# Normalised rows made, turned and stored in the message stage, and loaded as columns by the last stage

## The reference

```python
x = x + _L0_gnn_ref(_layernorm(x), edge_index, ...)
x = x + _L0_ffn_ref(_layernorm(x)[None], ...)[0]

def _L0_gnn_ref(x, ...):                       # H = 4 heads of C = 64, edges sorted by dst
    h = (x @ W).reshape(n, H, C)
    alpha = leaky_relu(a_src[src] + a_dst[dst])           # self loops included
    alpha = exp(alpha - segment_max(alpha, dst)[dst])
    alpha = alpha / (segment_sum(alpha, dst)[dst] + 1e-16)
    out = segment_sum(alpha[:, :, None] * h[src], dst) + bias
    return relu(layernorm(out) * ln_gamma + ln_beta)

def _L0_ffn_ref(x, ...):                       # B = 1: one routing decision for all rows
    logits = jnp.mean(x, axis=1) @ Wr + br     # the two best of 8 experts, for every row the same
    h = gelu(einsum('nd,edf->enf', x, W1) + b1)            # F = 512
    y = einsum('enf,efd->end', h, W2) + b2
    out = sum of the two chosen experts' y by their weights
    return layer_norm(out + x) * gamma + beta
```

## Time and profile before

| | |
|---|---|
| time, median of 3 runs (lowest, highest) | 3611.67 us (3609.06, 3613.48) |
| the profiled execution's own time | 3606.3 us |
| its span, first to last instruction | 3604.6 us |
| mean granted TensorE clock | 0.812 |
| PE busy | 2428.7 us (67%) |
| DVE busy | 2371.9 us (66%) |
| POOL busy | 1617.3 us (45%) |
| ACT busy | 1529.1 us (42%) |
| HBM read and written | 352.42 and 43.43 MB |

### The profile page before, as it was taken

How to read it: one execution, slowest core, us unless ns; L and a number is a source line. 1 busy time by engine, 2 the same in 40 slices (tenths; PEclk the granted TensorE clock), 3 DMA queues, 4 the chain that set the end, 5 groups by cost and what they waited for, 6 DMA issues and landing times. The chain is left out here.

```text
span 3604.6 us, 63268 instructions
## 1 busy us (share of the span) xinstructions
PE 2428.7 (67%) x12504; PEld 1741.4 (48%) x12504; DVE 2371.9 (66%) x9742; ACT 1529.1 (42%) x4803; POOL 1617.3 (45%) x1701
## 2 busy tenths in 40 slices
PE   8545556555665665665565556565565589999998
PEld 6434444444444444444444444444444356666666
DVE  6446766766766766766676766676676645566555
ACT  5334444544444544544444544444444321222211
POOL 0265665655665665665565655655655100000000
PEclk9857777777777777777877777777777799999999
DMA  7644444444444444444444444444444211111110
GB/s 206 191 119 125 130 126 124 128 125 125 127 128 123 130 127 124 128 128 124 127 127 125 129 124 126 132 122 124 134 125 122 48 56 35 35 35 35 41 41 32
DMA packets 237623, 397.71 MB, mean 110 GB/s; under 512 B 66609, under 2 KB 167729, under 8 KB 237425
## 3 DMA queue, kind: packets, MB, share of 16 engines
q0 software_dynamic: 80544, 229.59, 23.2%
q1 hardware_dynamic: 155674, 165.33, 15.0%
q10 hardware_dynamic: 1207, 1.09, 0.1%
HBM read 352.42 MB, written 43.43 MB: 110 GB/s over the span
## 5 line engine op out<-in xcount | busy, mean ns | idle before, releaser
L643 POOL DMA_INDIRECT rows<-table,idx x1666 | 1599.0, 960 | 1073.3 <-issue 471.5
L736 PE MATMUL bank<-msg,oh 128*128 128x260 f32 x3332 | 1091.9, 483 | 175.9 <-issue 125.4
L736 PEld LDWEIGHTS bank<-msg,oh 128*128 128x128 f32 x3332 | 789.1, 246 | 367.9 <-issue 205.2
L938 ACT ACTIVATE msg<-rows,we 128x65 f32<-128x65 f32 x1904 | 478.5, 333 | 0.4
L1195 DVE TENSOR_TENSOR msg<-rows,bank 128x520 f32<-128x520 f32 x595 | 377.2, 686 | 1.1 <-ACT carry L958 0.9
L756 PE MATMUL bank<-ident,lastmax 70*128 70x70 f32 x240 | 70.6, 388 | 403.8 <-DVE lastmax L1273 354.5
L829 PE MATMUL bank<-rows,msg 128*128 128x256 f32 x1536 | 340.6, 378 | 0.0
L816 PE MATMUL bank<-rows 128*128 128x512 f32 x768 | 336.3, 595 | 4.8 <-DMA rows<-in_L_ffn_W 4.8
L829 PEld LDWEIGHTS bank<-rows,msg 128*128 128x128 f32 x1536 | 288.4, 189 | 51.4 <-issue 10.6
L761 PE MATMUL bank<-ident_b,ohT 128*128 128x128 bf16 x1680 | 195.8, 306 | 161.6 <-DVE adsh L1297 69.1
L1009 ACT ACTIVATE ln<-mv,eps 128x1 f32<-128x1 f32 x119 | 35.1, 295 | 621.7 <-DVE mv L1344 454.3
(11 more groups left out here) (200 smaller groups left out, 3360.8 us busy)
## 6 DMA issues: line engine op xcount, KB each, us to landing
dst_b<-dst SPq DMA_DIRECT2D x122, 448.0 KB
rows<-table,idx POOLq DMA_INDIRECT x1666
tab_w<-table SPq DMA_DIRECT2D x121, 134.5 KB
x_w<-in_x_rows SPq DMA_DIRECT2D x121, 128.0 KB
x_mid<-x_o SPq DMA_DIRECT2D x119, 128.0 KB
table<-msg SPq DMA_DIRECT2D x50, 269.0 KB, 3.1
rows<-x_mid SPq DMA_DIRECT2D x26, 512.0 KB, 3.9
msg<-in_x_rows SPq DMA_DIRECT2D x51, 256.0 KB, 3.2
```

Of the source, the lines that this page charges most:

```text
L643: pool.indirect_dma_start(rows[:, slot, t, :], None, table, bass.IndirectOffsetOnAxis(ap=idx[slot][:, t:t + 1], axis=0), bounds_check=None ...
L736: mm = pe.matmul(psA, oh[:, of, t, :], msg[:, of, t, :], start=(t == 0), stop=(t == TILES - 1))
L938: ins = act.activation(head_cols(msg[:, s, t, :])[:, h, :], head_cols(rows[:, at.slot(), t, 0:HC1])[:, h, :], ACT.Copy, scale=we[:, t, h:h ...
```

## The change

Window by window, the message stage now makes the normalised rows itself (`xn`), turns them, and stores them as columns in a new HBM array `xn_t` (256 x 12,800). The last stage loads a group's columns from it in place of turning rows. The pieces of the diff are, in order: the lists of DVE, ACT and PE; the two PSUM places; XN on DVE; XNT on PE, behind `lastT^`, and a wait ahead of `router`; XNT on ACT, behind `oh*`; the store on SP, at the end of its step; and in the last stage the load on SP (one group ahead), PE's group, and DVE's copy.

```diff
-            wcur^ r_sc newseg^ r_mn node^ r_d1 r_d pen^ NODE_V* RUNMAX^ NOHAS* LASTMAX^ MTILE* ohT0^ MNODE* AD* MAXSELF* ohT^ ZN*
+            wcur^ r_sc newseg^ r_mn node^ r_d1 r_d pen^ NODE_V* RUNMAX^ NOHAS* LASTMAX^ XN MTILE* ohT0^ MNODE* AD* MAXSELF* ohT^ ZN*
...
-        act2 = Ticks(sem("act2"), """oh_b* we we_act carry msgs0 asrc^ msgs rexp acc carried oh* wself ln2 y2 lhs ln1 y1""", 6)
-        pe2 = Ticks(sem("pe2"), "nodemax* agg lT^ lastT^ turned^ expand* half router carry", 6)
+        act2 = Ticks(sem("act2"), """oh_b* we we_act ln2 y2 lhs carry msgs0 asrc^ msgs rexp acc carried oh* XNT wself ln1 y1""", 6)
+        pe2 = Ticks(sem("pe2"), "nodemax* agg lT^ lastT^ XNT turned^ expand* half router carry", 6)
...
+        psN = [bank[5][:, 512 - P:], bank[7][:, 512 - P:]]
...
+            def normed_rows(s):
+                return dve.scalar_tensor_tensor(out=xn[:, :], in0=x_o[:, s, 0:D], scalar=x_o[:, s, D:D + 1],
+                                                in1=ln2[:, 3:4].to_broadcast([P, D]), op0=ALU.subtract, op1=ALU.mult)
...
+                if before:
+                    act2.wait(dve, "y2", at)
+                    pe2.wait(dve, "XNT", at, -1)
+                mark(before, "XN", lambda: normed_rows(s))
...
+                if before:
+                    dve2.wait(pe, "XN", at)
+                    act2.wait(pe, "carry", at)
+                    act2.wait(pe, "XNT", at, -1)
+                    for k in range(KD):
+                        mm = pe.transpose(psN[k], xn[:, k * P:(k + 1) * P], ident[:, :])
+                    pe2.mark("XNT", mm)
...
+                if before:
+                    act2.wait(pe, "XNT", at)
...
+                if before:
+                    pe2.wait(act, "XNT", at)
+                    act.wait_ge(s_turned, at.k * (16 * RING) + 16 * (at.off - 2 + XPADS))
+                    for k in range(KD):
+                        ins = act.activation(xnT[:, k, :], psN[k], ACT.Copy)
+                    act2.mark("XNT", ins)
...
+            def store_turned(at, lead):
+                w = sp.value_load(step_tab[0:1, 0, bass.ds(at.number(lead), 1)], min_val=0, max_val=N)
+                sp.dma_start(xn_t[:, bass.ds(w, P)].rearrange("(k p) n -> p k n", p=P), xnT[:, :, :])\
+                  .then_inc(s_turned, 16)
...
+                if before:
+                    act2.wait(sp, "XNT", at)
+                    hold(sp, s_sp_held)
+                    store_turned(at, -2)
...
+            def load_transposed(at, lead):
+                sp.dma_start(fxT[:, at.slot(lead), :, :],
+                             xn_t[:, bass.ds(at.number(lead) * GROUP, GROUP)].rearrange("(k p) n -> p k n", p=P))\
+                  .then_inc(s_fxT[at.slot(lead)], 16)
...
             def group(at):
-                dve3.wait(pe, "xT", at, -1)
+                pe.wait_ge(s_fxT[at.slot()], at.landed(1))
...
-                    if q == QB // 2:
-                        pe3.mark("half", mm)
-                        transpose_rows(at, 1)
...
-            def move_transposed(at, lead):
-                s = at.slot(lead)
-                pe3.wait(dve, "xT", at, lead - 1)
-                for k in range(KD):
-                    ins = dve.tensor_copy(fxT[:, s, k, :], psF[k])
-                dve3.mark("xT", ins)
```

More of the change, by code:

```diff
@@ L144, in build @@
     XO_ROWS = (GROUPS + 1) * GROUP
+    XT_COLS = GROUPS * GROUP
+    XPADS = KD * -(-(XT_COLS - N) // D)
+    assert N + P <= XT_COLS and XPADS > 0
     with ExitStack() as ctx:
@@ L239, in build @@
         x_o = sb("x_o", [P, 2, D + 2])
+        xn = sb("xn", [P, D])
+        xnT = sb("xnT", [P, KD, P])
         zrow = sb("zrow", [1, D + 1])
@@ L306, in build @@
         s_mid = sem("s_mid")
+        s_turned = sem("s_turned")
+        s_fxT = [sem(f"s_fxT{i}") for i in range(2)]
         s_fwr = sem("s_fwr")
@@ L347, in build @@
         act3 = Ticks(sem("act3"), " ".join(HID), 2)
-        pe3 = Ticks(sem("pe3"), " ".join(HID) + " half xT out", 2)
+        pe3 = Ticks(sem("pe3"), " ".join(HID) + " out", 2)
         sp3 = Ticks(sem("sp3"), "stored", 3)
@@ L549, in _ @@
             step(over_last, -2, -1)
+            fin_act.wait(sp, "XNT", fin)
+            hold(sp, s_sp_held)
+            store_turned(over_last, -1)
+            load_transposed(At(0, 2, 0), 0)
             for slot in range(RING):
@@ L570, in _ @@
             hold(sp, s_sp_held)
+            sp.wait_ge(s_turned, total * 16 + 16 * XPADS)
+            hold(sp, s_sp_held)
             sp3.credit(sp)
@@ L763, in step @@
                 else:
-                    pe2.skip(pe, ["lT^", "lastT^", "turned^"], at)
+                    pe2.skip(pe, ["turned^"], at)
                 if ahead:
@@ L859, in _ @@
             pe.drain().then_inc(s_once, 1)
+            fin_dve.wait(pe, "XN", fin)
+            for k in range(KD):
+                mm = pe.transpose(psN_last[:, k * P:(k + 1) * P], xn[:, k * P:(k + 1) * P], ident[:, :])
+            fin_pe.mark("XNT", mm)
             pe.wait_ge(s_setup, N_MEAN)
@@ L889, in _ @@
                 act.dma_start(x_mid[r:r + n, :], zeros[0:n, :]).then_inc(s_tab[i] if i < PAIR_RING else s_pad, 16)
+            for c in range(N, XT_COLS, D):
+                n = min(D, XT_COLS - c)
+                for k in range(KD):
+                    act.dma_start(xn_t[k * P:(k + 1) * P, c:c + n], zeros[:, 0:n]).then_inc(s_turned, 16)
             act.wait_ge(s_pool, 6)
@@ L996, in step @@
                     act2.skip(act, ["oh*"], at)
+                if before:
+                    pe2.wait(act, "XNT", at)
+                    act.wait_ge(s_turned, at.k * (16 * RING) + 16 * (at.off - 2 + XPADS))
+                    for k in range(KD):
+                        ins = act.activation(xnT[:, k, :], psN[k], ACT.Copy)
+                    act2.mark("XNT", ins)
+                else:
+                    act2.skip(act, ["XNT"], at)
                 if prev:
@@ L1026, in _ @@
             fin_act.mark("lhs", act.activation(m_lhs[:, 0:1], mask[:, 2:3], ACT.Copy, scale=ln2[:, 3:4]))
+            fin_pe.wait(act, "XNT", fin)
+            act.wait_ge(s_turned, total * 16 + 16 * (XPADS - 1))
+            fin_act.mark("XNT", act.activation(xnT[:, :, :].rearrange("p k n -> p (k n)"), psN_last, ACT.Copy))
             for n in N_EXP:
@@ L1456, in _ @@
             step(over_last, -2, -1)
-            move_transposed(At(0, 2, 0), 0)
             dve3.rest(dve, DVE3_A)
+            fin_act.wait(dve, "y2", fin)
+            pe2.wait(dve, "XNT", over_last)
+            fin_dve.mark("XN", normed_rows(0))
             dve.wait_ge(s_once, 4)
```

52 lines of the change are left out of this document (27 added, 25 removed).

## The result

The changed kernel takes 3670.22 us (median of 4 runs, 3669.55 to 3672.44), the kernel before 3611.11 us (4 runs, 3609.06 to 3613.48). The ratio is 1.0165, 95% interval 1.0147 to 1.0182: 59 us slower, where 17 us less were forecast. The profiled execution has a span of 3667.8 us, 63.2 more than before.

The account below looks back on a forecast made before the run. PE was taken to bound the last stage, two late hand-offs between PE, POOL, DVE and ACT the message stage. 3606.3 - 20.9 + 2 + 1.5 = 3588.9, plus 5.4 to the median: 3594 us, range 3585 to 3660.

Parts of the forecast that it names:

- The last stage: PE loses eight transposes per group, 0.87 us each group for 24 groups: 20.9 us less; the added load costs nothing.
- the 468 us called DVE's: Last stage: DVE read as busy 468 of 710 us, so dropping its two copies gives nothing further.
- The costs of the single operations: Message stage: XN 0.48 us on DVE, XNT's transposes 0.22 or 0.44 on PE, its copies 0.25 each on ACT, hidden.
- So 0.48 fits: Message stage: XN's 0.48 us fits DVE's idle 0.70 us ahead of EDGE_V and 3.04 ahead of NODE_V; uncovered, +58 us.
- +2 us: Message stage: added work nearly all hidden, with 2 us taken for steps whose waits lie otherwise.
- Rival 1: Message stage: ACT sees PE's XNT late while gathers run, about +3.5 us per step, +410 us, 4004 us; chance 0.15.
- The sum of 22.4 us for POOL's step: Message stage: 14 gathers, some 17.5 us, plus standstills of 2.75 and 2.20 us, taken to account for the 21.98 us step.
- The store: Message stage: xnT is wanted again over 9 us after issue, against a 3.1 us landing for twice the size; no cost.
- Rival 2: Message stage: part of XN's 0.48 or ACT's 0.9 us shows, +18 us (3612) to +48 us (3642); chance 0.15.
- A rule against it: Message stage: a skill page says HBM writes can update the semaphore surprisingly late; that could eat the store's 9 us.

Follow-up runs that it names:

- e14: Kernel before with ACT's ln2, y2, lhs ahead of carry and XN behind LASTMAX^, no XNT or stores, late kind: 3643.91 us against 3616.67.
- e13: Changed kernel with XN in idle time ahead of DVE's wait for lT^, late kind: 3649.34 us against the kernel before's 3616.67.
- e8: Changed kernel without stores, zero transfers and their waits, last stage loading the input array, late kind: 3642.27 us against the kernel before's 3620.48.
- e7: Changed kernel with XN ahead of NODE_V but behind the wait for lT^, late kind: 3659.73 us against the kernel before's 3620.48.
- e4: Kernel before with only the new last stage, columns loaded from the input array, prompt kind: 3042.59 us against 3063.91.
- e5: Changed kernel unaltered, prompt kind: 3043.72 us against the kernel before's 3059.40.
- e9: Changed kernel with XN in idle time ahead of DVE's wait for lT^, prompt kind: 3055.37 us against the kernel before's 3064.90.
- e10: Changed kernel with XN in idle time, without stores, last stage loading from the input array, prompt kind: 3051.61 us against the kernel before's 3064.90.
- e1: Kernel before with only ACT's ln2, y2 and lhs moved ahead of carry, prompt kind: 3063.29 us against 3063.91.
- e3: Changed kernel without stores, zero transfers and their waits, last stage loading the input array, prompt kind: 3056.54 us against the kernel before's 3063.91.

## Why the prediction was wrong

On the late kind, from the least loss to the greatest (difference to before on the same chip; then the same with 20.0 us added back where the new last stage is in; POOL's idle time in the profiled execution). e14 and e13 share a chip, e8 and e7 share another; the lines of before and of the change are from the result. Each difference is good to about 6 us:

| kernel | against before, us | message stage and start, us | POOL idle, us |
|---|---|---|---|
| before | 0 | 0 | 1073.3 |
| e14: ACT's move, XN | +27 | +27 | 1118.4 |
| e8: and XNT | +22 | +42 | 1138.7 |
| e13: whole, XN in idle time | +33 | +53 | 1138.9 |
| e7: whole, XN ahead of NODE_V | +39 | +59 | 1149.0 |
| the change: whole | +59 | +79 | 1156.5 |

- **The last stage: right.** 0.87 us per group in the trace, -21.3 us alone in e4, -20.0 with the serial stretch in the result. One reading was wrong without consequence: the 468 us called DVE's are PE's weight loads; DVE had 415.36 us.
- **The costs of the single operations: right.** XN took 0.47 us, the copies 0.25 each, the transposes stood between `lastT^` and `turned^` as expected, ACT wasn't held and the store landed in time. XNT's two transposes on PE took about 0.32 us each (median over the trace), more than the 0.22 or 0.44 for both, and were hidden too. On the prompt kind the sum agrees, forecast -17.4, measured -15.7 (e5), but in part by luck: there POOL gathers without a pause, and the waits on which the prediction counted for cover play no part.
- **"So 0.48 fits", and with it "+2 us" for the message stage: the step that failed.** I had read that updates are acted on late while gathers run, but took the lateness as fixed in place, at `expand*` and `lT^`, and counted idle time ahead of EDGE_V and NODE_V as play. That time stood in the one step that was followed; 33 of the 118 steps had no such wait and took 20.0 us. Before, 40 steps were under 21.5 us, in the changed kernel 7. The runs show another rhythm, in which DVE's own results behind num are the late ones, DVE mostly starts a step behind POOL in place of ahead of it, and POOL waits longer. ACT's move and XN bring part of it (e14). The term of +2 us is 80.1 in the trace. That the late start of DVE is what makes POOL wait is read from the order of one step, not tested by a run.
- **The shares of the parts.** In medians, start and message stage together have +79: some 27 with ACT's move and XN, 15 more with XNT, 37 more with the stores. The last two shares are put together from three series of runs and are uncertain by that. On the chip of e13 and e14 alone, XNT and the stores with XN in idle time add 25 to the 27. Between the result and e13, XN's place is worth 26, again across series.
- **The reading behind it.** The prediction had ACT take `turned^`, ended at 669.29, only at 674.59, and DVE `expand*` only at 676.91. In the kernel before's timeline both engines first had other operations in their order, `ln1` and `y1` on ACT and the layer norm on DVE. So what these rows show of a late update is at most the last wait, 1.38 us at ACT and 0.70 at DVE. ACT's rows ahead of `oh_b`:

```profile
672.68 0.30 ACT L1009 ACTIVATE ln<-mv,eps 128x1 f32<-128x1 f32 x1 [3.75 <-DVE st L1341]
673.00 0.20 ACT L1011 ACTIVATE ln<-ln 128x1 f32<-128x1 f32 x1
```

Rival 1's +410 us rested on that reading. The sum of 22.4 us for POOL's step also counts the 0.30 us of issue twice at each pause.

- **The store: mis-sized.** Only its landing was priced, at nothing, and that was right. By the runs with and without it the store cost 17 us (e7 against e8, one chip, XN in two places) to 37 (the result against e8, from two series) through something else. That it does so by delaying updates or gathers is not shown; on the prompt kind e9 and e10, with and without it, differ by 3.8 us, within the noise.
- **Rival 2, "the play is partly used up", came nearest**: it had 0.4 us per step and 3642 as its upper case; measured are 0.68 us per step in the trace. What the prediction held against it, "behind that wait follow 2 to 3 us more", was the error above. Rival 1's form, a late update for ACT, didn't occur.
- **A rule against it**: the landing of the store held ACT for 0.3 us in the message stage and once for 2.53 us behind it. The Trainium skill, page Perfetto Trace Analysis, section DMA Instruction — HWDGE (DVE, Sync), warns that such a write to HBM can delay the semaphore surprisingly long. The one landing that this trace shows came 2.1 us behind its issue, with no gathers in flight; for the others it shows only that they were in time.

Open: how ACT's move and XN share the 27 us; whether any added work of this size brings the slower rhythm; what the stores cost on one and the same chip with nothing else changed; why a wait for DVE's own result is late for 3.3 us, and why only on some chips. No version was found that beats the kernel before on both kinds. On the prompt kind the change does (-15.7), and on the late kind XN in idle time loses 33 us (e13) where the change loses 59, not enough.

## What to carry to other kernels

Idle time in a step that waits on late updates need not be play, and one step need not stand for all: count how the steps differ, ask in which rhythm each stands, who of two engines starts it first, and what happens if a chain of dependent operations lands later in the run of transfers. Price a store among gathers by what its traffic does to the step, not by its landing alone, and with a run, since no row of before shows it. Run both kernels, and each variant, on the same chip: the sign of this change hangs on it, and shares of 10 or 20 us that are put together from several chips stay uncertain.

## What the runs showed of the hardware

- The same kernel takes 3609 to 3625 us in the result and with e7, e8, e13 and e14, and 3057 to 3068 us on four other chips. On the prompt kind only e1's kernel, which is as fast, has a trace; its transfers are the same as before's (237623 packets, 397.71 MB in both profiles). The message stage makes the difference, a step of 22.3 us or of 17.8. What differs in the traces is when an engine acts on an update: NODE_V waited 3.04 us in the earlier trace rows and not at all in e1's row, 225.0 against 98.5 us in all.
- On the prompt kind, ACT's move and XN made POOL's gathers 979 ns long in place of 957, +33 us, on two chips. With XNT beside them it was 963 (e3) or 959 (e5). POOL's own instruction was longer, with no wait in the profile; its cause wasn't tried.
